# One-hots of a later chunk between the adds of a chunk in a segment-sum GNN kernel

## The chip, the cores and the metric

The kernel runs on one NeuronCore of a Trainium2 chip. The metric is the device time of one execution in microseconds (us); less is better. The engines are named as in the profile: PE (TensorE), DVE (VectorE), ACT (ScalarE), POOL (GpSimd), SP (SyncE, which only issues transfers here). A q behind the name (DVEq) stands for the engine's sequencer: register, wait and branch instructions.

## What is computed

Two graph layers over 12,500 nodes of 128 features and 200,000 edges whose target nodes `dst` are sorted and lie denser at low numbers. Cut to what matters:

```python
# layer 0
h = relu(layernorm(x))
aggregated = segment_sum(edge_attr_64 @ W_edge.T, dst)          # 200000 edges -> 12500 nodes
aggregated = aggregated / clip(segment_sum(ones, dst), 1.0)[:, None]
x = x + concat([h @ W_self.T, aggregated @ W_neigh.T]) @ W_final.T + b_final
# layer 1
h = relu(layernorm(x))
agg = segment_sum(edge_attr_128, dst)
x = x + relu(concat([h, agg]) @ W1 + b1) @ W2 + b2
```

The kernel sums the raw edge rows first (they are linear in the weights) and multiplies by the weights per node.

## The kernel before

**Chunks.** The edges are cut into 128 chunks (`CH`) of 1,536 or 1,664 edges, that is 12 or 13 units of 128. A chunk's edges are summed with one-hot matrices: DVE compares the edges' places, relative to a window of 64 nodes, with 0..63 (`one_hots`, one instruction over all units of a chunk, L1011), and PE multiplies the edge rows of each unit by its one-hot (`sums`, L630, L632, L648, L657), which gives sums for a window of 64 nodes in a PSUM bank. Where edges are sparse, one window can't hold a whole chunk's targets, so a chunk is cut into batches with a window each. There are four zones of 32 chunks: 1 batch per chunk in zone 0, 2 in zone 1, 3 in zone 2, 4 in zone 3 (`PARTS`). The last chunk has 3.

**Adds.** `adds(t)` adds each batch's window from PSUM onto the running sums `agg` in SBUF, at a place known only at run time: one DVE instruction per batch (L1040), 319 in all. Consecutive windows can overlap, so each add waits for the one before it through the semaphore `s_added`. The places come from a table in SBUF (`base`): `load_bases` (L1018) loads one register for each two batches and unpacks it, on DVE's sequencer.

**Order.** Every engine's instructions are written out in ticks t = 0, 1, 2, ... of one chunk each. `ORDER` takes chunks from both ends: ticks 0 to 5 are zone 0; from tick 6 every even tick takes a chunk from the top (zone 3 up to tick 68, then zone 2) and every odd tick one from below (zone 0 to tick 27, zone 1 to tick 91, then zone 2); the last 15 ticks are dense chunks of zone 0. In one tick DVE does: node-group work that is due; `adds(t)`; a fold, if due (two instructions that move a wrapped window of 64 nodes, L1103 and L1105); `relative` for t < 3 (L992: places relative to the batch's first edge, for the next zone); `copy_table` for t = 1, 2, 3 (L999 to L1003: the transposed table of places of a zone, out of PSUM); and last `one_hots(t + 3)` (`AHEAD` = 3, four buffers). POOL adds up the units' one-hots for the degrees (`hot_sums(t + 2)`, L521), clears parts of `agg` (L507) and does adds for the node groups. PE does `sums(t)` and whatever node-group products are due. `sums(t)` waits for the adds of chunk t - 3 (three PSUM banks), for its one-hots, its `hot_sums` and its edge rows. The edge rows lie in five slots; SP issues the transfer for chunk t when `sums(t - 5)` is done.

**Start.** In ticks 0, 1 and 2, DVE's `relative` for a zone is followed on PE by that zone's table (`table`, L582: 12 or 13 transposes). PE's queue is in order, so `sums(t + 1)` stands behind it.

**Node groups.** When all edges of a group of 512 nodes are summed, at tick `TAKE[q]` (25 groups), PE multiplies that group's sums by the weights at the end of tick TAKE (`neigh`, L693). It waits for `s_added`: all adds up to those of tick TAKE - 1, and for a fold of the group. DVE's `layer_0` (L1111, L1114, L1119) follows in tick TAKE + 1, then statistics (L1128), normalisation on ACT (L902), PE's transposes (L668), the hidden layer (L705, L707), the output product (L714) and DVE's `result` (L1148) at the head of tick TAKE + 11. `own_part` (L677) on PE writes the same PSUM bank as the output product, and waits for DVE's `result` or ACT's copy `own` (L889) of its last use; the output product waits likewise.

Of the kernel before, what the change touches and what calls it, by code (L numbers as in the profile page):

```python
# [9 lines left out]
ALU = mybir.AluOpType  # L10
# [4 lines left out]
P = 128  # L15
# [4 lines left out]
WIN = 64  # L20
# [5 lines left out]
CH = 128  # L26
# [14 lines left out]
ZONES = (0, 3, 1, 2)  # L41
# [24 lines left out]
def batches_of(c):  # L66


    q = c // 32
    if c == CH - 1:  # L70
        return [(0, 3, P, 0), (3, 3, P, 1), (6, 1, H, 0)]
    kinds = ((2,), (0, 1), (0, 1, 2), (0, 1, 0, 1))[q]
    return [(b * RUNS[q], RUNS[q], P, kinds[b]) for b in range(PARTS[q])]


def build_gnn(nc, x, dst, edge_attr_128, edge_attr_64, W_self, W_neigh, W_edge, W_final, b_final,
# [161 lines left out]
    X_LEAD = 6  # L238
    WARM_UP = 5
    N_CONST = 10  # L240


    GP, GR = 125, 16
# [6 lines left out]
    with ExitStack() as ctx:  # L250
# [728 lines left out]
        def _(dve):  # L979
# [22 lines left out]
                else:  # L1002
                    nc.vector.tensor_copy(rel[:, q, 0:n, :], ps_tab(q)[:, 0:n, :]).then_inc(s_untab, 1)  # L1003

            def one_hots(t):
                c = ORDER[t]
                if t == 0:
                    dve.wait_ge(s_const, N_CONST)
                dve.wait_ge(s_untab, ZONES.index(c // 32) + 1)
                n = 7 if c == CH - 1 else RUNS[c // 32] * PARTS[c // 32]  # L1010
                nc.vector.tensor_tensor(onehot[:, t % HOTS, 0:n, :], iota_win[:, :].unsqueeze(1).to_broadcast([P, n, WIN]),  # L1011
                                        rel[:, c // 32, 0:n, c % 32].unsqueeze(2).to_broadcast([P, n, WIN]),
                                        ALU.is_equal).then_inc(s_hot, 1)

            def load_bases(c):
                nodes = []
                for k in range((len(batches_of(c)) + 1) // 2):
                    _, (both,) = nc.values_load_multi_w_load_instructions(  # L1018
                        base_pair[0:1, 2 * c + k:2 * c + k + 1], engines=DVE_ONLY, min_val=0, max_val=(SUMS - WIN - 1) * 65537,
                        skip_runtime_bounds_check_because="the table holds places among the sums")  # L1020
                    nodes += [(both & 65535).with_bounds(min_val=0, max_val=SUMS - WIN - 1),
                              (both >> 16).with_bounds(min_val=0, max_val=SUMS - WIN - 1)]
                return nodes

            def adds(t):
                c = ORDER[t]
                if t == 0:
                    dve.wait_ge(s_base, 5)
                nodes = load_bases(c)
                if t == 0 or cleared(t) > cleared(t - 1):  # L1030
                    dve.wait_ge(s_zero, 1 + cleared(t))
                dve.wait_ge(s_mm, t + 1)
                o = 0
                for i, (u0, R, K, kind) in enumerate(batches_of(c)):
                    planes = (slice(0, 2), slice(0, 3, 2), slice(0, 3))[kind]
                    w = 3 if kind == 2 else 2
                    if ADDED[t] + i:
                        dve.wait_ge(s_added, ADDED[t] + i)
                    here = agg[:, planes, bass.ds(nodes[i], WIN)]
                    nc.vector.tensor_tensor(here, ps[:, t % BANKS, o:o + w * WIN].rearrange("p (a n) -> p a n", a=w), here,  # L1040
                                            ALU.add).then_inc(s_added, 1)
                    o += w * WIN

            n0, n1, part = 12 * P, UNITS * P, LAST_E

# [118 lines left out]
            for t in range(1, AHEAD):  # L1164
# [10 lines left out]
            nc.vector.scalar_tensor_tensor(base[0:1, 0:SPLIT, :], wrapped[0:1, 0:SPLIT, :], float(FIRST_W), base[0:1, 0:SPLIT, :], ALU.add,  # L1175
                                           ALU.min).then_inc(s_base, 1)
            nc.vector.tensor_scalar(base[0:1, SPLIT:CH, :], wrapped[0:1, SPLIT:CH, :], float(UPPER_AT), None, ALU.add).then_inc(s_base, 1)
            for t in range(TICKS):
                for q in range(NG):
                    if t == TAKE[q] + 1:  # L1180
                        layer_0(q)
                    if t == TAKE[q] + 11:
                        result(q)
                    if t == TAKE[q] + 2:
                        stats_2(q)
                    if t == TAKE[q] + 4:
                        scale_2(q)
                for q in range(NG):
                    if t == SELF[q]:
                        stats_1(q)  # L1190
                    if t == SELF[q] + 2:
                        scale_1(q)
                if t < CH:
                    adds(t)
                    for i, (q, _) in enumerate(FOLDS):
                        if t == TAKE[q] - 1:
                            fold(i)
                    if t < 3:
                        relative(ZONES[t + 1])
                    if 1 <= t <= 3:  # L1200
                        copy_table(ZONES[t])
                    if t + AHEAD < CH:
                        one_hots(t + AHEAD)
                if t == 6:
                    check_bounds()
                if t == 8:
                    check_largest()
                if t == 10:
                    check_smallest()
                if t == 13:  # L1210
                    verdict()
# [107 lines left out]
```

## Time and profile before

| what | us |
|---|---|
| median of 3 runs | 573.98 |
| lowest and highest | 569.75, 574.9 |
| the profiled execution | 568.37 |
| its span, first to last instruction | 566.5 |
| PE busy | 507.7 (90%) |
| DVE busy | 403.6 (71%) |
| POOL busy | 360.5 (64%) |
| ACT busy | 152.8 (27%) |
| mean granted clock of PE | 0.964 of 2.4 GHz |

The table is read so: the span is what instructions fill; 1.9 us of the profiled execution's time lie around it. Durations of instructions come from this one execution. A busy time counts the engine's own datapath, not its sequencer. PE's share is the largest, and a busy PE is not at its peak; what an engine waited for stands in the rows further below.

### The profile page before, as it was taken

To read this page: it belongs to the slowest core of one execution; us is meant where nothing else is said; L and a number is where in the kernel's file an instruction comes from. 1 tells how busy PE (TensorE), PEld (TensorE's weight loads), DVE (VectorE), ACT (ScalarE), POOL (GpSimd) and SP (SyncE) were. 2 spreads that over 40 slices of the span, in tenths; PEclk is the share of its full clock that TensorE was granted. 3 is DMA by queue.
4 is the path that set the end of the run, shared out by engine and by line. 5 is a ranking of instruction groups with operands and counts; after the bars stand their busy time and mean duration, and the time that the engine had idled before them with its cause. 6 is when DMAs were issued, how large, how long until landed. Compare 5 with 4: busy or idle time off the path is not lost.

```text
span 566.5 us, 25890 instructions
## 1 busy us (share of the span) xinstructions
PE 507.7 (90%) x10989; PEld 453.1 (80%) x10989; DVE 403.6 (71%) x1166; ACT 152.8 (27%) x353; POOL 360.5 (64%) x524
## 2 busy tenths in 40 slices
PE   5568889899899998989989999998999879999893
PEld 5468788798788788878878887887888768988782
DVE  5554787887887877888786678878877866767321
ACT  0012012331414223332333224323422422223101
POOL 2637745777477675677867775784964773775730
PEclk9778899999999999999998999999999989999996
DMA  8946999999999999999997999998999976978910
GB/s 283 376 139 233 377 367 353 343 337 298 348 303 298 337 308 296 325 334 293 344 331 269 308 340 333 334 309 292 308 323 333 351 270 198 383 270 286 379 50 14
DMA packets 113229, 169.54 MB, mean 299 GB/s; under 512 B 5486, under 2 KB 84310, under 8 KB 113111
## 3 DMA queue, kind: packets, MB, share of 16 engines
q1 hardware_dynamic: 85843, 154.42, 78.5%
q10 hardware_dynamic: 27268, 13.43, 8.2%
q8 instruction: 89, 1.46, 1.0%
q14 instruction: 29, 0.24, 0.1%
HBM read 161.43 MB, written 6.40 MB: 296 GB/s over the span
## 4 chain that ended last, share of the span: by engine, by line
PE 53%; DVE 31%; issue 8%; DVEq 5%; POOL 1%; DMA 1%; ACT 0%; ACTq 0%; POOLq 0%
PE ps L630 18%; PE ps L648 10%; DVE onehot L1011 9%; DVE agg L1040 7%; PE ps L693 6%; PE ps L632 3%; PE ps L677 3%; PE ps L705 3%; PE ps L668 3%; DVEq L1040 3%; PE ps L707 2%; PE ps L714 2%; DVEq L1018 2%; DVE bn L1083 2%; DVE x L1119 2%
## 5 line engine op out<-in xcount | busy, mean ns | idle before, releaser
L630 PEld LDWEIGHTS ps<-onehot,ring 128*64 128x64 f32 x3126 | 199.0, 141 | 31.6 <-issue 23.3
L630 PE MATMUL ps<-onehot,ring 128*64 128x64 f32 x3126 | 217.9, 228 | 6.4 <-issue 4.3
L632 PE MATMUL ps<-onehot,ring 128*64 128x64 f32 x3126 | 218.2, 228 | 3.9 <-issue 3.8
L521 POOL TENSOR_TENSOR hot_part<-onehot 128x384 bf16<-128x384 f32 (+2 forms) x128 | 111.7, 873 | 171.8 <-DVE onehot L1011 168.5
L632 PEld LDWEIGHTS ps<-onehot,ring 128*64 128x64 f32 x3126 | 199.1, 141 | 4.6 <-issue 4.6
L1040 DVE TENSOR_TENSOR agg<-ps,agg 128x128 f32 (+1 forms) x319 | 97.1, 304 | 128.1 <-PE ps L657 51.6
L1011 DVE TENSOR_TENSOR onehot<-iota_win,rel 128x768 f32<-128x768 f32 (+2 forms) x128 | 147.3, 1151 | 0.4
L648 PE MATMUL ps<-onehot,ring 128*64 128x64 f32 x3126 | 121.5, 225 | 7.1 <-issue 6.7
L648 PEld LDWEIGHTS ps<-onehot,ring 128*64 128x64 f32 x3126 | 108.7, 140 | 6.8 <-issue 6.5
L693 PEld LDWEIGHTS ps<-w_c,agg 128*128 128x128 f32 x424 | 51.1, 196 | 10.8 <-DVE agg L1040 6.2
L693 PE MATMUL ps<-w_c,agg 128*128 128x129 f32 x424 | 53.5, 280 | 6.7 <-DVE agg L1040 4.9
L521 POOL TENSOR_TENSOR hot_sum<-hot_part 128x128 bf16<-128x128 bf16 x96 | 49.1, 511 | 7.5
L902 ACT ACTIVATE h<-x,nmr,rstd 128x128 f32<-128x128 f32 x98 | 40.4, 483 | 36.4 <-DVE nmr L1140 36.3
L874 ACT ACTIVATE hn<-x,nmr,rstd 128x128 f32<-128x128 f32 x98 | 40.4, 483 | 24.7 <-DVE nmr L1095 24.5
L499 POOL TENSOR_TENSOR x<-x,b_bc 128x512 f32<-128x512 f32 (+1 forms) x25 | 34.2, 1370 | 10.2 <-ACT h L902 10.2
L917 ACT ACTIVATE hid<-ps,b_col 128x512 f32<-128x512 f32 (+1 forms) x25 | 17.0, 679 | 80.7 <-PE ps L707 76.9
L677 PE MATMUL ps<-w_a,hT 128*128 128x128 f32 x196 | 30.2, 300 | 7.0 <-DVE x L1148 7.0
L507 POOL MEMSET agg<- 128x1536 f32 (+2 forms) x26 | 35.4, 1365 | 0.0
L521 POOL TENSOR_TENSOR hot_sum<-hot_sum,hot_part 128x128 bf16<-128x128 bf16 x64 | 30.8, 481 | 5.0
L889 ACT COPY own<-ps 128x512 f32<-128x512 f32 (+1 forms) x25 | 14.5, 579 | 71.7 <-PE ps L677 56.1
L486 POOL TENSOR_TENSOR x<-x,b_bc 128x512 f32<-128x512 f32 (+1 forms) x25 | 33.0, 1321 | 0.0
L714 PE MATMUL ps<-w,hid 128*128 128x128 f32 x196 | 29.4, 294 | 3.9 <-ACT own L889 3.4
(118 smaller groups left out, 570.5 us busy)
## 6 DMA issues: line engine op xcount, KB each, us to landing
ring<-in_edge_attr_dram SPq DMA_DIRECT2D x95, 768.0 KB, 5.4
ring<-in_edge_attr_dram SPq DMA_DIRECT2D x96, 384.0 KB, 6.8
ring<-in_edge_attr_dram SPq DMA_DIRECT2D x32, 832.0 KB, 6.0
ring<-in_edge_attr_dram SPq DMA_DIRECT2D x32, 416.0 KB, 7.4
x<-in_x_dram ACTq DMA_DIRECT2D x23, 256.0 KB, 6.3
out_dram<-x ACTq DMA_DIRECT2D x23, 256.0 KB
x<-in_dst_dram SPq DMA_DIRECT2D x1, 384.0 KB
x<-in_dst_dram SPq DMA_DIRECT2D x1, 208.0 KB, 3.5
```

What stands on the lines that cost most here:

```text
L507: nc.gpsimd.memset(agg[:, :, a:b], 0.0).then_inc(s_zero, 1)
L521: nc.gpsimd.tensor_tensor(out, a, b, ALU.add).then_inc(s_hotsum, 1)
L630: nc.tensor.matmul(bank[0:H, o:o + WIN], ring128[0:K, slot, u, 0:H], hots, start=u == 0, stop=r == R - 1, skip_group_check=True)
L632: nc.tensor.matmul(bank[H:P, o:o + WIN], ring128[0:K, slot, u, H:D], hots, start=u == 0, stop=r == R - 1, skip_group_check=True)
L648: nc.tensor.matmul(bank[feats, o:o + WIN], ring64[0:K, slot, u, :], onehot[0:K, hot, u, :], start=False, stop=True, skip_group_check=True)
L677: last = nc.tensor.matmul(ps_row[:, j * D:(j + 1) * D], hT[:, j * P:(j + 1) * P], w_a[:], start=True, stop=True)
L693: last = nc.tensor.matmul(ps_nb[:, j // 2, j % 2, :], agg[:, 1 + k, a + j * P:a + (j + 1) * P], w_c[:, k, :], start=i == 0, stop=i == len( ...
L714: last = nc.tensor.matmul(ps_row[:, j * D:(j + 1) * D], hid[:, j * P:(j + 1) * P], w2[:], start=True, stop=True)
L874: last = nc.scalar.activation(hn[:, j, :], x0[:, j0 + j, :], ACT.Relu, bias=nmr1[:, u, j:j + 1], scale=rstd1[:, u, j:j + 1])
L902: last = nc.scalar.activation(h2[:, j, :], x0[:, j0 + j, :], ACT.Relu, bias=nmr2[:, u, j:j + 1], scale=rstd2[:, u, j:j + 1])
L1011: nc.vector.tensor_tensor(onehot[:, t % HOTS, 0:n, :], iota_win[:, :].unsqueeze(1).to_broadcast([P, n, WIN]), rel[:, c // 32, 0:n, c % 32] ...
L1040: nc.vector.tensor_tensor(here, ps[:, t % BANKS, o:o + w * WIN].rearrange("p (a n) -> p a n", a=w), here, ALU.add).then_inc(s_added, 1)
```

## The change

`one_hots(t + 3)` moves from the end of DVE's tick into `adds(t)`: it stands behind the first add. In chunks of 3 or 4 batches it is cut into two instructions of half the units each, behind the first and behind the second add. `load_bases` of chunk t + 1 stands behind the first add and the first part of the one-hots, instead of ahead of the adds of tick t + 1. `copy_table` of ticks 1, 2 and 3 moves behind the first add too, ahead of the one-hots. Folds, and `relative` in ticks 0 to 2, stay behind `adds(t)`, and so now stand behind the one-hots (and `copy_table`) of their tick. Nothing else changes: buffers, counts of semaphores and the other engines' programs are the same.

```diff
--- before.py
+++ after.py
@@ -238,6 +238,7 @@
     X_LEAD = 6
     WARM_UP = 5
     N_CONST = 10
+    COPIED_AT = (1, 2, 3)
 
 
     GP, GR = 125, 16
@@ -1002,15 +1003,17 @@
                 else:
                     nc.vector.tensor_copy(rel[:, q, 0:n, :], ps_tab(q)[:, 0:n, :]).then_inc(s_untab, 1)
 
-            def one_hots(t):
+            def one_hots(t, part=0, parts=1):
                 c = ORDER[t]
                 if t == 0:
                     dve.wait_ge(s_const, N_CONST)
                 dve.wait_ge(s_untab, ZONES.index(c // 32) + 1)
                 n = 7 if c == CH - 1 else RUNS[c // 32] * PARTS[c // 32]
-                nc.vector.tensor_tensor(onehot[:, t % HOTS, 0:n, :], iota_win[:, :].unsqueeze(1).to_broadcast([P, n, WIN]),
-                                        rel[:, c // 32, 0:n, c % 32].unsqueeze(2).to_broadcast([P, n, WIN]),
-                                        ALU.is_equal).then_inc(s_hot, 1)
+                a, b = n * part // parts, n * (part + 1) // parts
+                made = nc.vector.tensor_tensor(onehot[:, t % HOTS, a:b, :], iota_win[:, :].unsqueeze(1).to_broadcast([P, b - a, WIN]),
+                                               rel[:, c // 32, a:b, c % 32].unsqueeze(2).to_broadcast([P, b - a, WIN]), ALU.is_equal)
+                if part == parts - 1:
+                    made.then_inc(s_hot, 1)
 
             def load_bases(c):
                 nodes = []
@@ -1020,17 +1023,17 @@
                         skip_runtime_bounds_check_because="the table holds places among the sums")
                     nodes += [(both & 65535).with_bounds(min_val=0, max_val=SUMS - WIN - 1),
                               (both >> 16).with_bounds(min_val=0, max_val=SUMS - WIN - 1)]
-                return nodes
+                return nodes[:len(batches_of(c))]
 
             def adds(t):
+
                 c = ORDER[t]
-                if t == 0:
-                    dve.wait_ge(s_base, 5)
-                nodes = load_bases(c)
                 if t == 0 or cleared(t) > cleared(t - 1):
                     dve.wait_ge(s_zero, 1 + cleared(t))
                 dve.wait_ge(s_mm, t + 1)
                 o = 0
+                nodes = places[t]
+                parts = 0 if t + AHEAD >= CH else 1 if len(nodes) < 3 else 2
                 for i, (u0, R, K, kind) in enumerate(batches_of(c)):
                     planes = (slice(0, 2), slice(0, 3, 2), slice(0, 3))[kind]
                     w = 3 if kind == 2 else 2
@@ -1040,6 +1043,12 @@
                     nc.vector.tensor_tensor(here, ps[:, t % BANKS, o:o + w * WIN].rearrange("p (a n) -> p a n", a=w), here,
                                             ALU.add).then_inc(s_added, 1)
                     o += w * WIN
+                    if i == 0 and t in COPIED_AT:
+                        copy_table(ZONES[COPIED_AT.index(t) + 1])
+                    if i < parts:
+                        one_hots(t + AHEAD, i, parts)
+                    if i == 0 and t + 1 < CH:
+                        places[t + 1] = load_bases(ORDER[t + 1])
 
             n0, n1, part = 12 * P, UNITS * P, LAST_E
 
@@ -1175,6 +1184,8 @@
             nc.vector.scalar_tensor_tensor(base[0:1, 0:SPLIT, :], wrapped[0:1, 0:SPLIT, :], float(FIRST_W), base[0:1, 0:SPLIT, :], ALU.add,
                                            ALU.min).then_inc(s_base, 1)
             nc.vector.tensor_scalar(base[0:1, SPLIT:CH, :], wrapped[0:1, SPLIT:CH, :], float(UPPER_AT), None, ALU.add).then_inc(s_base, 1)
+            dve.wait_ge(s_base, 5)
+            places = {0: load_bases(ORDER[0])}
             for t in range(TICKS):
                 for q in range(NG):
                     if t == TAKE[q] + 1:
@@ -1197,10 +1208,6 @@
                             fold(i)
                     if t < 3:
                         relative(ZONES[t + 1])
-                    if 1 <= t <= 3:
-                        copy_table(ZONES[t])
-                    if t + AHEAD < CH:
-                        one_hots(t + AHEAD)
                 if t == 6:
                     check_bounds()
                 if t == 8:
```

## Rows read from the trace of the kernel before

**Rows 1.** The page, busy time by engine, and the chain's shares:
```profile
PE 507.7 (90%) x10989; PEld 453.1 (80%) x10989; DVE 403.6 (71%) x1166; ACT 152.8 (27%) x353; POOL 360.5 (64%) x524
...
PE 53%; DVE 31%; issue 8%; DVEq 5%; POOL 1%; DMA 1%; ACT 0%; ACTq 0%; POOLq 0%
```

**Rows 2.** The waits of PE: who for whom, us in total, times, longest:
```profile
PE ps L582 <- DVE x L992: 12.8, 4, 6.6
PE ps L677 <- DVE x L1148: 7.0, 5, 2.5
...
PE ps L693 <- DVE agg L1040: 4.9, 5, 1.6
...
PE ps L714 <- ACT own L889: 3.4, 1, 3.4
...
PE ps L693 <- issue: 1.8, 1, 1.8
```

**Rows 3.** The waits of DVE, same columns:
```profile
DVE agg L1040 <- PE ps L657: 51.6, 37, 5.4
DVE agg L1040 <- DVE agg L1040: 37.9, 191, 0.6
DVE agg L1040 <- issue: 28.0, 56, 1.1
DVE deg L1111 <- PE ps L693: 10.3, 10, 2.3
```

**Rows 4.** Timeline of DVE in mid-run: start, us, line, form, idle before:
```profile
243.25 0.29 DVE L1040 TENSOR_TENSOR agg<-ps,agg 128x128 f32 x1 [0.19 <-DVE agg L1040]
243.46 0.95 DVE L1011 TENSOR_TENSOR onehot<-iota_win,rel 128x768 f32<-128x768 f32 x1
```

**Rows 5.** The line of the loads of places, ns min/median/max:
```profile
L1018 DVEq TENSOR_LOAD <-base x192: 299/306/745, 19.2 to 550.8; - x192
```

**Rows 6.** Timeline of DVE, one-hots with nothing between them and the adds:
```profile
457.00 0.95 DVE L1011 TENSOR_TENSOR onehot<-iota_win,rel 128x768 f32<-128x768 f32 x1
457.87 0.28 DVE L1040 TENSOR_TENSOR agg<-ps,agg 128x128 f32 x1
```

**Rows 7.** One-hots by form and by line: busy, mean ns; min/median/max ns:
```profile
L1011 DVE TENSOR_TENSOR onehot<-iota_win,rel 128x768 f32<-128x768 f32 x95 | 110.3, 1161 | 0.1
L1011 DVE TENSOR_TENSOR onehot<-iota_win,rel 128x448 f32<-128x448 f32 x1 | 0.6, 616 | 0.0
...
L1011 DVE TENSOR_TENSOR onehot<-iota_win,rel x128: 616/1016/2081, 9.7 to 544.2; 128x768 f32<-128x768 f32 x95, 128x832 f32<-128x832 f32 x32, 128x448 f32<-128x448 f32 x1
```

**Rows 8.** Timeline of DVE, ticks 0, 1 and 2:
```profile
22.20 1.03 DVE L1011 TENSOR_TENSOR onehot<-iota_win,rel 128x832 f32<-128x832 f32 x1
...
30.31 0.56 DVE L999 COPY rel<-ps 128x384 f32<-128x384 f32 x1
...
31.09 1.03 DVE L1011 TENSOR_TENSOR onehot<-iota_win,rel 128x832 f32<-128x832 f32 x1
...
39.67 0.56 DVE L1003 COPY rel<-ps 128x384 f32<-128x384 f32 x1
```

**Rows 9.** Timeline of PE, the second of the three tables:
```profile
30.34 1.82 PE L582 MATMUL ps<-ident,x 32*128 32x32 f32 x12 [2.40 <-DVE x L992]
```

**Rows 10.** The chain in order of time, before the longest wait for `result`:
```profile
296.14 0.69 DVE x L1148
296.97 2.04 PE ps L677 x8
```

**Rows 11.** Busy time of stretches; the column behind POOL's is the granted clock:
```profile
296.90:300.40 3.50, 3.43 (x24) 3.13 (x26) 2.88 (x7) 0.50 (x2) 2.53 (x4) 0.51 0.99 342
...
464.20:467.60 3.40, 3.40 (x19) 3.40 (x18) 0.87 (x2) 1.04 (x4) 3.15 (x6) 0.50 0.59 191
```

**Rows 12.** Timeline of all engines, what leads to the wait for `own`:
```profile
458.03 0.73 POOL L521 TENSOR_TENSOR hot_part<-onehot 128x256 bf16<-128x256 f32 x1 [2.32 <-DVE onehot L1011]
...
462.93 0.58 ACT L889 COPY own<-ps 128x512 f32<-128x512 f32 x1 [4.39 <-POOL x L493]
```

## Prediction

> **What bounds the kernel now.** I read the busy times and the chain first, then the waits of PE, then those of DVE, then timelines of DVE and windows around the longest waits. The reader is to see that PE is the resource that runs out: 507.7 of 566.5 us busy, and 53% of the chain that ended last. DVE has 403.6 us of work but 31% of the chain, with 5% more on its sequencer [rows 1]. A chain that passes through an engine with 29% free time means that this engine falls behind in places and is waited for there. So an edit to DVE alone can win at most what PE waits for DVE, and the waits of PE give that directly [rows 2]: 12.8 us in the start, where tables wait for `relative` (L992); 7.0 us in five places where `own_part` waits for `result` (L1148); 4.9 us in five places where a group's products (L693) wait for the last add, and 1.8 us in one place ("issue") where the missing thing is the fold; and 3.4 us once for ACT's copy `own`, itself late because of POOL. Without the start the sum is 7.0 + 4.9 + 1.8 + 3.4 = 17.1 us.
>
> Two of these waits cost more than themselves. Behind the 2.5 us wait at L677 and behind the 3.4 us wait at L714 the granted clock is 0.51 and 0.50 for about 3.4 us, the level of 1.2 instead of 2.4 GHz, after PE had stood still [rows 11]. Work that takes 3.4 us at half speed takes 1.7 at full speed, so the two cost 3.4 us together. The ceiling of what mid-run can give is then about 20 us.
>
> **What DVE saves.** Four terms.
> First, the gap between adds. Each add waits for the one before, 191 times for 37.9 us, 0.20 us each [rows 3]. With a one-hot in between, the earlier add is long done. The first gap of every chunk with 2 or more batches goes, and the second of those with 3 or 4: 96 + 64 = 160 of 191, 31.7 us.
> Second, the loads of places. A load takes 0.31 us [rows 5], and a chunk of 3 or 4 batches has two. Where a whole one-hot runs just ahead of the add, they are hidden: the add at 457.87 starts without any gap behind a one-hot of 0.95 us [rows 6]. Where short group work stands in between, the add waits: 28.0 us in 56 places ("issue") [rows 3]. With the loads a tick early, that goes. But behind half a one-hot two loads aren't covered: two loads and about 0.2 us of unpacking (the gap of a following add, which contains the same unpacking) are 0.8 us against 0.47, in the 20 ticks from 92 on in which zone 2 follows zone 2. That is 20 x 0.35 = 7 us back.
> Third, a new gap. With the one-hots gone from the end of a tick, the first add of the next tick stands directly behind the last add of this one, unless group work lies between. That is up to 95 ticks x 0.2 = 19 us; group work stands in about half of the ticks, so I take 9.
> Fourth, the split. 448 elements took 0.616 us and the shortest of 768 about 0.95 (the row of mid-run), so 320 elements cost 0.33 and an instruction has a fixed part of 0.16 [rows 4, 7]. The one-hot starts at 243.46, 0.08 before the add ahead of it ends at 243.54 [rows 4], so a part of this is hidden by overlap. 64 extra instructions cost 64 x 0.08 to 0.16 = 5 to 10 us; I take 6.
> The sum is 31.7 + 28.0 - 7 - 9 - 6 = 38 us over the 113 ticks that are not tail, 0.33 us per tick of about 4.
>
> At the split a rule can be weighed. The trace's fixed part is 0.16 us, of which overlap hides half. The Trainium skill, "VectorE: DVE Perf Modes", section on the TRN2 errata, says that a fixed latency is exposed between SBUF-source instructions and advises tiles of at least 512 elements; halves of 384 go against it. By its measured fixed term of about 150 cycles at 0.96 GHz the 64 instructions would cost 10 us as an estimate, and the room would be 34 instead of 38.
>
> **What becomes of PE's waits.** `result` stands at the head of a tick, so it comes earlier by all that DVE saved since it last waited for PE. Ahead of the longest wait, `result` on DVE from 296.14 is what PE's L677 at 296.97 waits for [rows 10]. The stretches ahead of these waits are 3 to 9 ticks long, worth 1 to 3 us against waits of 0.5 to 2.5. I take 5.5 of the 7.0 us.
> The last add of a tick is another matter. It now stands behind the one-hots: 0.95 us plus half a split, less one or two gaps of 0.2, is 0.7 us later within its tick. Against that stands what was saved in the 3 to 6 ticks before, 1.0 to 2.0 us. A fold stays behind the last add. So the 4.9 + 1.8 = 6.7 us at L693 fall to about 4.0, and groups whose last add was just in time begin to wait: DVE itself waited for L693 in 10 of 25 groups [rows 3], so there it is ahead; of the others a few may lose up to 0.7 each, I take 1.5. Net gain 1.2.
> The wait for `own`: POOL stood waiting for a one-hot until 458.03, and its queue is in order, so the add whose end ACT's copy waits for was late by that [rows 12]. A one-hot that comes 1.5 to 2 us earlier moves all of it; I take 1.9 of 3.4.
> The two long waits shrink by about half or more, and I take it that the two stretches at half clock behind them go too: 3.4 (the bounds are 0 and 3.4).
> Mid-run gains 5.5 + 1.2 + 1.9 + 3.4 = 12.0 us.
>
> **What the start loses.** In ticks 0, 1 and 2 PE waits for `relative` directly: the wait of 2.40 us ahead of the table at 30.34 ended with L992 [rows 9]. Behind that table stand `sums` of the next tick, its adds, and the next `relative`, so the three waits are in series. `relative` now stands behind the one-hots and the copy of its tick. Tick 0: 1.03. Tick 1: the copy, from 30.31 to the one-hot at 31.09, is 0.78, and the one-hot 1.03. Tick 2: 0.56 + 0.03 + 1.03 [rows 8]. Sum 4.5 us. No work covers it: the transfers wait for slots that `sums` frees, so they move along. From below the bound is 4.2 (the instructions alone); from above, one more stretch of 3.4 us at half clock while PE stands idle longer, 6.2.
>
> **The sum.** -12.0 + 4.5 = -7.5 us. Against the profiled execution's 568.4 that is 560.9. This execution lies under all three timed runs, whose median is 573.98; in proportion (-1.3%) I predict 566.4 there. For the unknown parts, mid-run can give from 3 (only `result` improves, by half, and the clock stays) to 17 us, so the likeliest case by itself reaches from -1 to -13 us, 561 to 573.
>
> **Costed at nothing.** The registers held over a tick and the extra waits on the sequencer run beside the one-hots. One-hots that are ready earlier gain nothing on PE in themselves: the waits of PE have one wait for a one-hot, in the start. Edge transfers are not moved.
>
> **The rivals.**
> *The last add decides (slower).* Every group's products wait for an add that comes 0.7 us later. The five waits of today show that this point is tight; DVE being ahead at 10 groups speaks against it. If the 15 other groups pay 0.7 each, that is 10.5 us, against 5.5 from `result` and 1.9 from `own`, plus 4.5 for the start and no clock regained: +1.7; if DVE's room is also only half, as when the start's idle time costs clock and the new gaps come in all ticks, `result` gives 2.5 and `own` 1: +7 to +8, about 581. It decides from the point where DVE saves less than 0.15 us per tick, because then five ticks don't repay 0.7.
> *The port (no change).* One-hots of 768 elements take 1.16 us in the mean and up to 2.08 against 0.95 for the undisturbed [rows 7], so 0.2 us of each is lost to something. If each of the 64 extra instructions meets the same, DVE's room falls by 13 to 25 us, and the mid-run gain to about two thirds, 8: the net is -3.5, 570.5. The Trainium skill, "SBUF — State Buffer", gives a mechanism in its part on the shared port pair: a VectorE instruction with two SBUF inputs and a GpSimd instruction that reads SBUF exclude each other for a whole instruction. The trace has the long one-hots, but does not name their cause.
> *The gains only move (no change).* PE, relieved of a wait, runs into the next limit a few ticks on, POOL or its own queue. Mid-run gives 4 to 5 and the start takes them: 574.
> *It does not do what it says.* The loads could fail to overlap, if the sequencer held them until the one-hot's end. Then 28 us of DVE's idle time stay, the room is 10 to 15 us and the time 575 to 580. [Rows 6] speak against it.
>
> **How the numbers follow.** The forecast has 0.48, the port 0.12, the gains only move 0.22, the last add 0.12, no overlap 0.06. The measurement tells about 1% from no change. Faster by over 1% is most of the forecast and a little of better cases: 0.47. Slower by over 1% is most of the last add and part of no overlap: 0.14. The rest is 0.39. The range takes the likeliest case and both no-change cases, down to -16 us and up to +5: 558 to 579.
>
> **What would show it.** In the changed kernel: the wait of L1040 for L1040 down from 37.9 to some 15 us, its "issue" down from 28 to under 10; PE's wait for L992 up from 12.8 to about 17; its wait for L1148 under 2; its wait at L693 no more than now; half one-hots of about 0.55 us, and no stretch at half clock behind 296. I am wrong if PE's waits at L693 grow by more than `result` gives back, or if PE's busy time, which should stay at 505 to 508, moves.

## The result, and the profile after

| | before | after |
|---|---|---|
| median of 4 runs, us | 573.24 | 556.81 |
| lowest to highest | 569.75 to 574.9 | 553.76 to 559.7 |
| the profiled execution | 568.37 | 556.97 |
| its span | 566.5 | 555.1 |

The ratio is 0.972, with a 95% interval of 0.965 to 0.979: 2.8% faster, where 1.3% was forecast, and 1.2 us under the low end of the range. A second session with the changed kernel gave 0.978 (0.973 to 0.982), 557.3 against 570.6. Ratios and intervals, here and below, leave out the runs that fell in the slower of two states that executions of a kernel show; medians are of all runs.

The page of the changed kernel, busy time by engine and the chain's shares. Lines are shifted: one-hots are L1013, adds L1043, products L694, `own_part` L678, `result` L1157, nmr L1149, tables L583, `relative` L993.

```profile
PE 503.9 (91%) x10989; PEld 450.1 (81%) x10989; DVE 390.6 (70%) x1230; ACT 151.5 (27%) x353; POOL 368.4 (66%) x524
...
PE 81%; issue 6%; DVE 4%; DVEq 1%; ACT 0%; POOL 0%
```

DVE and its sequencer have gone from 36% of the chain [rows 1] to 5%. The chain is PE's own work. The waits of PE (who for whom, us in total, times, longest), then those of DVE, of the changed kernel:

```profile
PE ps L583 <- DVE x L993: 16.1, 4, 6.7
...
PE ps L694 <- issue: 2.3, 2, 1.4
...
PE ps L694 <- DVE agg L1043: 1.1, 3, 0.6
PE ps L678 <- DVE x L1157: 1.0, 2, 0.7
...
PE ps L678 <- issue: 0.7, 1, 0.7
```
```profile
DVE agg L1043 <- PE ps L658: 95.9, 73, 7.0
DVE deg L1120 <- PE ps L694: 19.5, 17, 3.1
DVE agg L1043 <- issue: 14.0, 18, 7.1
DVE agg L1043 <- DVE agg L1043: 6.4, 33, 0.3
```

Against [rows 2]: the wait for `result` went from 7.0 to 1.0 us, those at the products from 6.7 to 3.4, the one for `own` from 3.4 to nothing, and the one for `relative` grew from 12.8 to 16.1. Of the 3.4 us at the products only 1.1 are surely a wait for an add: the 2.3 marked issue, and the 0.7 at `own_part`, each came 0.8 to 1.5 us behind a packet of the instruction queue, as the standstills in the last section do, so they may not be waits for DVE at all. Against [rows 3]: the adds wait for each other 33 times instead of 191, and DVE now waits for PE at its adds 73 times instead of 37: it is ahead. One of the 18 gaps marked issue, 7.1 us long, is a wait in the start under another name, so 6.9 us are left of 28.0.

The timeline of DVE in the changed kernel, one chunk of zone 3 and the tick behind it:

```profile
239.95 0.29 DVE L1043 TENSOR_TENSOR agg<-ps,agg 128x128 f32 x1 [2.21 <-PE ps L658]
240.15 0.55 DVE L1013 TENSOR_TENSOR onehot<-iota_win,rel 128x384 f32<-128x384 f32 x1
240.62 0.28 DVE L1043 TENSOR_TENSOR agg<-ps,agg 128x128 f32 x1
240.82 0.55 DVE L1013 TENSOR_TENSOR onehot<-iota_win,rel 128x384 f32<-128x384 f32 x1
241.29 0.28 DVE L1043 TENSOR_TENSOR agg<-ps,agg 128x128 f32 x1
241.76 0.29 DVE L1043 TENSOR_TENSOR agg<-ps,agg 128x128 f32 x1 [0.19 <-DVE agg L1043]
241.97 0.17 DVE L1147 RECIPROCAL rstd<-std 128x4 f32<-128x4 f32 x1
242.17 0.30 DVE L1149 SCALAR_TENSOR_TENSOR nmr<-mv,rstd 128x4 f32<-128x4 f32 x1
```

Two of the three gaps are gone; each one-hot starts 0.08 to 0.09 before the end of the add ahead of it, and each add behind one 0.08 before its end.

And the start, DVE in tick 1 of the changed kernel, and PE at the third table:

```profile
29.89 0.36 DVE L1043 TENSOR_TENSOR agg<-ps,agg 128x192 f32 x1 [6.42 <-PE ps L658]
30.16 0.55 DVE L1000 COPY rel<-ps 128x384 f32<-128x384 f32 x1
30.75 0.15 DVE L1002 COPY rel<-ps 64x1 f32<-64x1 f32 x1
30.82 1.01 DVE L1013 TENSOR_TENSOR onehot<-iota_win,rel 128x832 f32<-128x832 f32 x1
31.86 1.75 DVE L993 TENSOR_TENSOR x<-x,firsts 32x1536 f32<-32x1536 int32 x1
```
```profile
44.21 1.64 PE L583 MATMUL ps<-ident,x 32*128 32x32 f32 x12 [3.80 <-DVE x L993]
```

The third table starts at 44.2 instead of 39.7. The first product of tick 3 on PE, in the kernel before and in the changed one:

```profile
42.42 0.37 PE L630 MATMUL ps<-onehot,ring 128*64 128x64 f32 x1
```
```profile
46.94 0.37 PE L631 MATMUL ps<-onehot,ring 128*64 128x64 f32 x1
```

### The profile page after: what moved, and what is told of

It reads as the page before. It is cut to its first block, busy times and chain, and to the rows that moved or that the text cites. A ratio compares the mean times of both kernels' runs of the same rounds, so it can differ in the third digit from the quotient of the medians.

```text
span 555.1 us, 25952 instructions
## 1 busy us (share of the span) xinstructions
PE 503.9 (91%) x10989; PEld 450.1 (81%) x10989; DVE 390.6 (70%) x1230; ACT 151.5 (27%) x353; POOL 368.4 (66%) x524
## 4 chain that ended last, share of the span: by engine, by line
PE 81%; issue 6%; DVE 4%; DVEq 1%; ACT 0%; POOL 0%
PE ps L631 28%; PE ps L649 15%; PE ps L694 9%; PE ps L706 5%; PE ps L633 5%; PE ps L678 5%; PE ps L669 4%; PE ps L715 4%; PE ps L708 4%; DVE agg L1043 2%; PE ps L658 1%; DVE x L1157 1%; DVE onehot L1013 1%; DVE bn L1137 0%; DVEq L1043 0%
## 5 line engine op out<-in xcount | busy, mean ns | idle before, releaser
L522 POOL TENSOR_TENSOR hot_part<-onehot 128x384 bf16<-128x384 f32 (+2 forms) x128 | 116.7, 912 | 152.3 <-DVE onehot L1013 150.6
L1043 DVE TENSOR_TENSOR agg<-ps,agg 128x128 f32 (+1 forms) x319 | 95.0, 298 | 120.1 <-PE ps L658 95.9
L1013 DVE TENSOR_TENSOR onehot<-iota_win,rel 128x384 f32<-128x384 f32 (+3 forms) x192 | 164.5, 857 | 0.2
L694 PEld LDWEIGHTS ps<-w_c,agg 128*128 128x128 f32 x424 | 49.8, 191 | 7.3 <-DVE agg L1043 3.7
L694 PE MATMUL ps<-w_c,agg 128*128 128x129 f32 x424 | 52.3, 276 | 3.3 <-issue 2.3
L522 POOL TENSOR_TENSOR hot_sum<-hot_part 128x128 bf16<-128x128 bf16 x96 | 44.7, 466 | 7.5
L500 POOL TENSOR_TENSOR x<-x,b_bc 128x512 f32<-128x512 f32 (+1 forms) x25 | 35.6, 1424 | 10.2 <-ACT h L903 10.2
L522 POOL TENSOR_TENSOR hot_sum<-hot_sum,hot_part 128x128 bf16<-128x128 bf16 x64 | 34.9, 545 | 5.0
L487 POOL TENSOR_TENSOR x<-x,b_bc 128x512 f32<-128x512 f32 (+1 forms) x25 | 34.2, 1369 | 0.0
L883 ACT COPY hT<-ps 128x512 f32<-128x512 f32 (+1 forms) x25 | 14.5, 579 | 70.5 <-PE ps L669 70.5
L494 POOL TENSOR_TENSOR x<-x,own 128x512 f32<-128x512 f32 (+1 forms) x25 | 31.9, 1275 | 0.0
```

Source lines behind the costliest of these rows:

```text
L487: nc.gpsimd.tensor_tensor(rows, rows, b0_bc[:, :].unsqueeze(1).to_broadcast([P, nt, D]), ALU.add).then_inc(s_xb, 1)
L500: nc.gpsimd.tensor_tensor(rows, rows, b2_bc[:, :].unsqueeze(1).to_broadcast([P, nt, D]), ALU.add).then_inc(s_x1b, 1)
L522: nc.gpsimd.tensor_tensor(out, a, b, ALU.add).then_inc(s_hotsum, 1)
L694: last = nc.tensor.matmul(ps_nb[:, j // 2, j % 2, :], agg[:, 1 + k, a + j * P:a + (j + 1) * P], w_c[:, k, :], start=i == 0, stop=i == len( ...
L1013: made = nc.vector.tensor_tensor(onehot[:, t % HOTS, a:b, :], iota_win[:, :].unsqueeze(1).to_broadcast([P, b - a, WIN]), rel[:, c // 32, a ...
```

## The experiments

Each is compared with the kernel before in its own session (medians there between 570.3 and 571.5). The ratios are known to 0.4 to 0.9%, so a difference of 2 or 3 us between two kernels is within the noise. In the table at the end of this section the medians stand together.

**The kernel before again.**

> The kernel before once more, unchanged, to see how its executions differ among themselves. The changed kernel's profiled execution (556.97 us) was 11.4 us under that of before (568.37), but its median 16.4 us under. Theory 'spread': the first profiled execution of before was one of its luckier ones, by fewer or shorter standstills of PE; then this run's profile should lie at 570 to 575 and show 2 to 6 us more in waits of PE or in stretches at half clock than the first, in places that move from run to run. Rival 'outside the span': the span is 566 to 567 again and the rest of the time lies around it.

570.6 us, ratio 0.999 (0.995 to 1.003); its span was 571.9, 5.4 us over the first. PE's waits of this profile:

```profile
PE ps L648 <- issue: 11.7, 14, 2.1
PE ps L677 <- DVE x L1148: 7.3, 5, 2.6
PE ps L630 <- issue: 6.3, 6, 2.5
```

The waits for `result` are the same. What moved are PE's standstills inside a chunk, marked issue (11.7 and 6.3 against 6.7 and 4.3 us in the first profile), and the stretches at half clock: two more of 3.4 us after tick 12. So the profile on which I forecast was one of the faster executions, 2 to 3 us under the medians of the later sessions, and 573.2, the median beside the first result, is the slowest of all. Spread of this size is enough for the difference between the gain in the first pair of profiles, 11.4 us, and those in the medians of two sessions, 16.4 and 13.3.

**Relative first**, twice, the second time beside the changed kernel.

```diff
 here = agg[...]; nc.vector.tensor_tensor(...)          # the add
+if i == 0 and t < 3:
+    relative(ZONES[t + 1])
 if i == 0 and t in COPIED_AT:
     copy_table(...)
```

> The changed kernel, but in ticks 0 to 2 relative stands right behind the first add, ahead of copy_table and the one-hots, as it did before. The theory of the start (three tables of PE wait in series for relative, 4.5 us of the wait are the moved work) expects PE's wait for relative back from 16.1 to about 12.8 us and the time 4.5 to 6 us under the changed kernel, about 551.5. The rival (the start is absorbed later, by transfers or by DVE catching up) expects under 2 us.

> relative first, once more, beside the changed kernel itself. The start theory expects 4 to 5 us under the changed kernel in the same session, PE's wait for relative near 12.5 against 16; the rival (absorbed later) under 2 us. The first look had only 2 us between the medians of two sessions, and 3.7 us between the profiled spans.

554.6, and in the second session 554.4 against the changed kernel's 557.3: 2.9 us. The wait for `relative` went from 16.4 to 11.9. In the trace PE's chunk of tick 3 starts 4.5 us later in the changed kernel than in before (46.9 against 42.4). So the trace shows the loss that was forecast at the start. At the end 2.9 us are seen; with intervals of 0.5% on each ratio this is apart neither from the whole 4.5 nor from the rival's under 2.

**The changed kernel again.**

> The changed kernel once more, unchanged, in the same session as the next three, as their yardstick. From its first profile and the kernel before run twice, the change is worth 14 to 16 us, so a ratio of 0.973 to 0.976. Theory 'clock': in the two profiles of before PE ran at half clock in 2 and 4 stretches of 3.4 us after tick 12, in the changed one in none; then none or one shows again. Rival 'luck of one profile': 2 or more show.

557.3, and again no stretch at half clock between 64 and 544 us. 'Clock' holds for both profiles of each kernel.

**No split.**

```diff
-parts = 0 if t + AHEAD >= CH else 1 if len(nodes) < 3 else 2
+parts = 0 if t + AHEAD >= CH else 1
```

> The changed kernel with the one-hots whole behind the first add in all chunks, nothing else changed: 64 instructions fewer, but the second gap of the 64 chunks with 3 or 4 batches is open again (64 x 0.20 = 13 us of DVE) and the two loads are hidden again behind a whole one-hot (7 us back). Theory 'room' (only DVE's spare time counts; split costs 6, saves 13 less 7): DVE's room changes by 0 to 2 us, the time by less than 1 us. Rival 'position' (what counts is when the last add comes or when the first half is ready): the time moves by over 3 us.

557.2, no difference. The gaps between adds are back to 19.4 us (13 more) and DVE's busy time is down by 7 against the first profile of the changed kernel and by 13 against the second: the split pays for itself, as expected, and neither costs nor gives in the time.

**Loads late.**

> The changed kernel, but the places of a chunk are loaded at the head of its own tick, as before. Theory 'room': the 28 us of gaps marked issue come back on DVE, for about half of what DVE saved, so PE's waits for DVE in mid-run go from 5 back to 8 or 10 us and the time rises by 3 to 5 us, to about 561. Rival 'gaps alone': the gaps between adds did it all, and the time stays within 1 us of the changed kernel.

558.9, ratio 0.976 (0.967 to 0.985): 1.6 to 2 us over the changed kernel, less than expected and within the noise. The gaps marked issue are back (22.9 us without the one in the start), and PE's waits in mid-run rose only from 4 to 7 us. Of these, 6.0 stand at the products.

**One more instruction** in each tick, short and long (its own semaphore is left out of the excerpt).

```diff
 adds(t)
+if 4 <= t < 113:
+    nc.vector.memset(wrapped[0:1, :, :], 0)      # e5; in e6 tensor_scalar(wrapped, wrapped, 0.0, add)
```

> The changed kernel with one more DVE instruction behind the adds of each tick from 4 to 112: a memset of one partition, about 0.3 us, 109 x 0.3 = 33 us, nearly all that DVE saved, without touching the order of adds, loads and one-hots. Theory 'room': PE's waits for DVE, ACT and POOL in mid-run come back, at least half of what was saved: +6 to +12 us over the changed kernel. Rival 'position' (one-hots earlier for POOL, loads earlier): the added time lies in DVE's idle time and the kernel slows by under 3 us.

> The changed kernel with a longer extra DVE instruction behind the adds of ticks 4 to 112 (an add of 0 to 512 int16 elements of one partition, about 0.6 us, so 60 us and more in all, against about 20 of the shorter one). DVE then has as much to do as before the change, in the changed order. Theory 'room': the time goes back to that of before plus the 4.5 us of the start, 568 to 577, with PE's waits for DVE at 15 us or more. Rival 'order': it stays under 562.

The short one took 272 ns and 29.6 us in all: 557.6, ratio 0.975 (0.969 to 0.982), no difference in the time, where I had expected 6 to 12 us. Its waits of PE:

```profile
PE ps L695 <- DVE agg L1044: 2.0, 3, 1.0
...
PE ps L695 <- issue: 1.8, 2, 1.3
...
PE ps L679 <- DVE x L1158: 1.5, 2, 1.0
```

The long one took 717 ns in the mean, 78 us in all: 570.0, ratio 0.998 (0.994 to 1.001), the time of before. Its waits of PE:

```profile
PE ps L679 <- DVE x L1158: 6.4, 5, 2.8
...
PE ps L695 <- issue: 4.1, 4, 2.2
...
PE ps L695 <- DVE agg L1044: 3.1, 3, 1.3
...
PE ps L716 <- ACT own L891: 1.7, 1, 1.7
```

With the changed order kept and only DVE's spare time taken away, the same waits are back, 15.3 us of them. So spare time is what the gain in mid-run comes from. But the first 30 us of instructions, 18 to 24 us of occupied time in the table below, cost nothing that can be seen.

**One-hots first.**

```diff
+if 4 <= t < 113:
+    one_hots(t + AHEAD)
 dve.wait_ge(s_mm, t + 1)
```

> The changed kernel, but from tick 4 to 112 the whole one-hots stand ahead of the adds of their tick, ahead of the wait for PE's sums too: the gaps between adds are open again (38 us), the loads stay hidden, and the last add of a tick still stands behind the one-hots. Theory 'room': where DVE is early the one-hots fill its wait, so the loss is a part of 31 us: +2 to +6 us over the changed kernel. Rival 'last add': PE's waits at the groups' products grow by up to 0.7 us at each group, +8 us or more. If DVE has more spare time than needed, under 1 us.

556.5, no difference, although all 191 gaps are back (49.3 us); I had expected a loss of 2 to 6 us. PE's waits at the products:

```profile
PE ps L694 <- DVE agg L1045: 1.0, 1, 1.0
```

This is not quite the test of the last add that it was meant to be: ahead of the wait for PE's sums the one-hots fill time in which DVE would stand idle, so where DVE is early the last add is not moved at all. In the kernels with one-hots between the first and the last add, early loads and no long extra instruction, the waits at the products are 2.3 to 5.4 us.

**One part alone: loads early, one-hots where they were.**

```diff
 if t + AHEAD < CH:
     one_hots(t + AHEAD)
+if t + 1 < CH:
+    places[t + 1] = load_bases(ORDER[t + 1])
```

> The kernel before with one part of the change alone: the places of chunk t + 1 are loaded behind the one-hots at the end of tick t. Order of adds and one-hots as before, so the gaps between adds stay (38 us). Theory 'room': DVE wins the 25 to 28 us marked issue, more than half of what it needs, and the kernels with part of the room back (loads late: 558.9, one more instruction: 557.6) cost only 1 to 2 us over the changed one; with no loss at the start this should then give 556 to 562. Rival 'order' (what counts is that POOL's sums no longer run beside DVE's short instructions behind the one-hots): PE's waits for DVE and POOL stay near 15 us and the time at 566 to 569.

552.2, ratio 0.967 (0.961 to 0.972): 19 us, where 9 to 15 were expected, and more than the whole change, at least in part since the start is not touched. PE's and DVE's waits of this kernel:

```profile
PE ps L677 <- DVE x L1146: 2.2, 3, 1.1
...
PE ps L693 <- DVE agg L1038: 1.5, 2, 0.8
```
```profile
DVE agg L1038 <- DVE agg L1038: 37.2, 191, 0.3
...
DVE agg L1038 <- issue: 1.7, 4, 0.7
```

**The other part alone: one-hots between the adds, loads late, relative first.**

> The one-hots between the adds (split as in the change), but the places loaded at the head of their own tick as before, and relative right behind the first add in ticks 0 to 2, so that the start loses nothing. Theory 'room, with a floor' (over the kernels so far, the time without the start's loss is 552 to 554 wherever DVE's busy time plus its own gaps is under 437 us, and rises from there): this has about 427 us, so 553 to 556, nearly the whole gain, though loads early alone gave the whole gain too. Rival 'loads only': the one-hots between the adds are worth little, and the time is 562 to 570.

556.5, ratio 0.973 (0.968 to 0.977). Each part alone gives most of the gain; together they don't add up. The waits of PE that are left stand almost all at the products:

```profile
PE ps L694 <- issue: 4.8, 2, 2.5
PE ps L694 <- DVE agg L1044: 4.5, 4, 2.4
...
PE ps L678 <- DVE x L1158: 1.3, 2, 1.1
```

That is 9.3 us at the products, 6.8 without the longer one marked issue, which came 1.4 us behind a packet of the instruction queue. Before had 6.7. So the products gained nothing, while `result` fell from 7.0 to 1.3. A last add that comes later behind one-hots and late loads would do this; it was not tested by itself.

**The scale steps moved** in the kernel before. In its trace the short nmr instruction ran beside POOL's first sum of the same one-hots (DVE, then POOL):

```profile
244.53 0.97 DVE L1140 SCALAR_TENSOR_TENSOR nmr<-mv,rstd 128x4 f32<-128x4 f32 x1
```
```profile
244.49 1.00 POOL L521 TENSOR_TENSOR hot_part<-onehot 128x384 bf16<-128x384 f32 x1 [0.89 <-DVE onehot L1011]
```

They end within 0.01 us of each other. So it is throughout: each of the 22 nmr of this line that took over 0.3 us ended 0.01 to 0.03 us behind an instruction of POOL. In the changed kernel adds, which read PSUM, stand there instead. nmr comes later in POOL's sum and took 0.30 us in the timeline above.

```diff
-if t == TAKE[q] + 4: scale_2(q)      # at the head of the tick; scale_1 likewise
 adds(t)
+if t == TAKE[q] + 4: scale_2(q)
 one_hots(t + AHEAD)
```

> The kernel before, with only the two short scale steps (reciprocal and nmr, L1138 and L1140 and their twins) moved from the head of the tick, right behind the one-hots of the last one, to behind the adds and ahead of the one-hots. In before, nmr took 811 ns in the mean beside POOL's first sum of the same one-hots, in the changed kernel 435. Theory 'port': nmr falls to 300 to 400 ns, DVE wins 9 us of busy time, and the time falls by 2 to 5 us. Rival (nmr's duration has another cause, or 9 us are too few to be seen): nmr stays near 800, or the time stays within 1.5 us.

nmr, min/median/max in ns, in before and in this kernel:

```profile
L1140 DVE SCALAR_TENSOR_TENSOR nmr<-mv,rstd x25: 160/970/1028, 96.4 to 557.1; 128x4 f32<-128x4 f32 x24, 128x2 f32<-128x2 f32 x1
```
```profile
L1140 DVE SCALAR_TENSOR_TENSOR nmr<-mv,rstd x25: 160/221/1286, 98.0 to 547.8; 128x4 f32<-128x4 f32 x24, 128x2 f32<-128x2 f32 x1
```

The median fell from 970 to 221 ns, DVE's busy time from 403.6 to 381.4 us, and the time to 559.9, ratio 0.981 (0.976 to 0.987): 11.5 us, more than twice what I expected. Of the 22 us of busy time 14 are nmr and its twin of layer 0, and 8.5 are the one-hots, which fell from 1151 to 1085 ns in the mean; why these fell was not tested. Moving the steps also changes when ACT gets them, so the 11.5 us are not all proved to be the 22 us of busy time.

**The start.**

```diff
+relative(ZONES[1])                   # ahead of the one-hots of chunks 1 and 2
 for t in range(1, AHEAD): one_hots(t)
 ...
-if i == 0 and t < 3: relative(ZONES[t + 1])
+if i == 0 and t < 2: relative(ZONES[t + 2])
```

> The changed kernel with every relative one tick earlier: the one of the second zone ahead of the one-hots of chunks 1 and 2 in the start, those of the third and fourth behind the first add of ticks 0 and 1. PE's tables then find their rows ready. The start theory (three waits in series, 16 us with the first) expects PE's wait for relative at 3 to 6 us, of which about 8 to 10 us reach the end: 547 to 549. The rival (the start is held by something else, the base table or clock) expects 554 or more, as with relative first.

542.1, ratio 0.949 (0.944 to 0.954): 12 us under relative first, more than the 5 to 7 expected, and the best kernel here with the next two. PE waits 3.5 us for `relative` instead of 12. Most of the rest goes with the clock: busy times of the start (PEclk is the column behind POOL's), relative first and then this kernel:

```profile
16.00:60.00 44.00, 31.50 (x605) 29.64 (x604) 22.54 (x46) 5.83 (x12) 25.17 (x87) 0.69 0.67 242
```
```profile
16.00:50.00 34.00, 28.74 (x626) 26.66 (x624) 23.42 (x48) 5.84 (x12) 29.24 (x89) 0.85 0.94 337
```

About as many matmuls (626 and 605) were done in 10 us less, at a mean clock of 0.85 instead of 0.69, and PE's busy time for them is 2.8 us shorter.

**Loads early, and whole one-hots between the adds, both with this start.**

> The kernel before with the places loaded a tick early (552.2 alone) and every relative one tick earlier in the start, which took the changed kernel with relative first from 554.4 to 542.1. One-hots at the end of the tick as before, none split. Theory 'room, with a floor': DVE has enough room without the one-hots between the adds, so 539 to 542. Rival 'every bit counts': DVE's gaps of 37 us between adds cost again, 545 or more.

> The kernel with relatives early in the start (542.1), with the one-hots whole behind the first add. Without the start's mend the split made no difference (557.2 against 557.3). Theory 'room, with a floor': 541 to 543. Rival (the half one-hots meet POOL more often, 745 ns each against 550 undisturbed, and this shows now that the start is short): 539 or less.

543.2 (0.953) and 542.1 (0.948). With the start mended the order of adds and one-hots makes no measurable difference.

**All together.** DVE's occupied time is its busy time, plus the waits of adds for adds, plus those marked issue (without the one of 3 to 7 us in the start that some kernels have). PE's waits are those for `result`, at the products (marked issue too) and for `own`. Kernels marked * have the start's loss, those marked + the mended start.

| kernel | DVE: busy + adds + issue | occupied | PE waits | median |
|---|---|---|---|---|
| before | 403.6 + 37.9 + 28.0 | 470 | 17.1 | 573.2 |
| before again | 401.3 + 37.9 + 24.9 | 464 | 14.8 | 570.6 |
| e6 * | 453.3 + 5.9 + 5.3 | 465 | 15.3 | 570.0 |
| e9 | 381.4 + 38.2 + 23.8 | 443 | 7.0 | 559.9 |
| e11 + | 401.3 + 37.2 + 1.1 | 440 | 4.6 | 543.2 |
| e4 | 399.6 + 37.2 + 1.7 | 439 | 3.7 | 552.2 |
| e5 * | 414.2 + 5.9 + 7.6 | 428 | 5.3 | 557.6 |
| e7 * | 375.3 + 49.3 + 0 | 425 | 1.0 | 556.5 |
| e10 | 392.0 + 6.5 + 22.7 | 421 | 10.6 | 556.5 |
| e3 * | 390.7 + 6.5 + 22.9 | 420 | 7.3 | 558.9 |
| e12 + | 387.1 + 19.4 + 4.8 | 411 | 6.4 | 542.1 |
| after again * | 397.0 + 6.4 + 6.1 | 410 | 3.5 | 557.3 |
| e2 * | 383.8 + 19.4 + 5.2 | 408 | 3.6 | 557.2 |
| e8 + | 395.9 + 6.4 + 5.9 | 408 | 2.6 | 542.1 |
| e1 again | 394.8 + 6.4 + 6.9 | 408 | 3.3 | 554.4 |
| e1 | 394.2 + 6.4 + 6.2 | 407 | 4.5 | 554.6 |
| after * | 390.6 + 6.4 + 6.9 | 404 | 4.4 | 556.8 |

Up to about 440 us occupied no loss can be seen (552 to 559 without the mended start, with all the rest that differs, and 542 to 543 with it); above that stand 560 at 443 and 570 at 464. But the total is not the whole of it: e4 and e9 lie 4 us apart and differ by nearly 8 us in the time. e10 and e3 have the longest waits of the lower half without the mended start, and 9.3 of 10.6 and 6.0 of 7.3 us of these are at the products (2.5 and 3.1 of them behind a packet of the instruction queue). These two have one-hots between the adds and late loads, which both stand ahead of a tick's last add; whether this is the reason is open. Open too is why e6, which still carries the loss in the start, is no slower than before at the same occupied time; it had one stretch at half clock in mid-run, before had two and four.

## Why the prediction was wrong

The step that failed is what becomes of PE's waits, and there the size of two terms: the gain at the products, put at 1.2 us, was 3.3, and the gain at the wait for `own`, put at 1.9, was 3.4. The mechanism, a DVE with more spare time for which PE waits less, was right.

- **What bounds the kernel**: right. PE's waits for the others were the ceiling, 17.1 us and 3.4 for the clock. PE's busy time was 503.9 and 501.5 us in the two profiles, under the 505 to 508 that I had given as a sign. That sign contradicted my own sum, which takes 3.4 us of half clock out of the 507.7 and so expects 504.3.
- **What DVE saves**: the gaps between adds fell from 37.9 to 6.4 (forecast 31.7, measured 31.5) and those marked issue to 6.9 (forecast 28 less 7 left). The new gap at the tick's end, 9 us, did not come: DVE is ahead there and waits for PE anyway. The split costs 7 to 13 us of busy time by e2, where I had 6. DVE's busy time fell by 13 us all the same, for which the forecast had no term: nmr and its twin take 10 us less (nmr 811 to 435 ns), and the one-hots, whose durations rose by 17 us (147.3 to 164.5), overlap with the adds at more seams. Room was 38 us by forecast and 60 to 66 by the trace (470 against 410 and 404). The error is large, but it is not what failed: e5 has about the room that I forecast (428 against 470 and 464), and PE's waits there are nearly as short as in the changed kernel.
- **What becomes of PE's waits**: this step failed, in size. `result`: 5.5 us forecast, 6.0 measured (5.5 in e5). Products: 1.2 forecast, 3.3 measured (2.9 in e5), and 5.6 if the 2.3 us marked issue are not DVE's. `own`: 1.9 forecast, 3.4 measured (3.4 in e5). Clock: 3.4, as forecast from two stretches. These come to 16.1 us instead of 12.0. At the products I had charged 0.7 us at each group for the last add behind the one-hots, and 1.5 us for groups that would begin to wait. In the changed kernel PE waits for an add at three groups, 1.1 us in all. The shift may not be free, by e10, but with the loads early the saving outweighs it nearly everywhere. For each wait I had set the mean saving per tick, 0.33 us, against its length; e4 and e5 show that nearly all waits are gone with 31 to 42 us of the first profile's 470 saved, by whichever part.
- **What the start loses**: right to 0.1 us in the trace (42.4 to 46.9 for PE's chunk of tick 3); at the end 2.9 us were measured, which the noise does not tell from 4.5.
- **The sum**: 16.1 less 4.5 is 11.6 us, and the two profiles differ by 11.4, where I had 7.5. The rest of the miss, from 11.4 to 16.4, is in the yardsticks, and partly chance. I took the share from a profile of 568.4, among the faster of this kernel; the second has two more stretches at half clock and longer standstills. And I applied it to 573.98, the slowest median of this kernel: with the second session's ratio of 0.978 it would give 561, inside the range. The low end, 16 us, was the ceiling of 20.5 less the start, so the range left no room for this. There is also a slip in the range of the likeliest case: a gain of 3 less 4.5 in the start is a loss of 1.5 us, not a gain of 1.
- **The rivals**: *the last add decides* fell in the changed kernel, whose waits at the products are 3.4 us and not more than before; e10, where they did not fall, is the one sign of the effect. Its price was summed wrong: 10.5 less 5.5 and 1.9, plus 4.5, is 7.6 and not 1.7, and in the second case 11.5 and not 7 to 8. *The port* was right that split one-hots run longer (745 ns in the mean, 550 undisturbed) and wrong on the sign of the whole: the order removed a collision elsewhere. *The gains only move* and *no overlap* fell with the changed kernel's waits.

## What to carry to other kernels

Here the engine at 90% waited now and then for one at 70%, and the gain from lightening that helper was closer to a step than to a slope: a saving of some 30 us in 470 gave nearly the whole, by either of two parts, and what was saved beyond it gave nothing that could be measured. Where waits look like these, price the change at nearly the whole of them once the saving is well past what the worst stretch lacks, and look for the cheapest saving that gets there (here a few lines that load registers one tick early). Test it with a dose: the same kernel with a useless instruction per tick. And when something is moved in a queue, look at the short start loop too: here mending three handovers in series, and the clock with them, gave 2%. Last, take a second profile and a second median of the kernel before ahead of a forecast to the microsecond.

## What the runs showed of the hardware

**A standstill of PE with no wait behind it.** In each profile PE stands still 11 to 20 times in the middle of a chunk, 0.4 to 2.5 us each. One of them in the kernel before, and what the transfer queues carried in a window of 1.4 us around it:

```profile
97.97 0.22 PE L630 MATMUL ps<-onehot,ring 128*64 128x64 f32 x1
...
100.69 0.27 PE L630 MATMUL ps<-onehot,ring 128*64 128x64 f32 x1 [2.49 <-issue]
```
```profile
q1 hardware_dynamic: 298, 0.49, 97.7%
q8 instruction: 1, 0.02, 4.9%
```

By the trace's records a packet of 16 KB on the instruction queue lay from 98.2 to 99.3, beside 298 packets of edge rows. In both profiles of before and the first of after, every standstill marked issue of 0.4 us and more had such a packet ending 0.8 to 1.6 us before PE went on, except one ahead of a group's products in each profile of before. There are 88 or 89 such packets in a run, one in 6 us, so this is hardly chance; most of them are followed by no standstill. That the program's code comes late because it queues behind data is argued from this, not tested. PE's waits marked issue sum to 17 to 23 us in all kernels, and with the start mended they are the largest wait of PE that is left.

**A shared way between DVE and POOL.** A 128x4 instruction took 970 ns in the median beside a POOL sum that reads SBUF, and 221 when moved. The Trainium skill, "SBUF — State Buffer", part on the shared port pair, says that a VectorE instruction with two SBUF inputs and a GpSimd instruction that reads SBUF exclude each other for a whole instruction. The trace agrees: the two ended within 0.01 us of each other, and all 22 long ones within 0.03. I had named this rule for the one-hots alone.
